# Recurrence with attention: both gates as separate tanh of ScalarE on the weighted sums

## The reference, cut to what matters

```python
def step(h, x_t):                                   # h: [B, 128], 512 steps in order
    combined = concat([h broadcast, enc_hiddens])   # [B, 77, 256]
    score = tanh(combined @ W_att) @ V_att          # [B, 77]
    attn = softmax(score)
    context = attn @ enc_hiddens                    # [B, 128]
    gz, gr, gh = split(concat([x_t, context]) @ Wi + b, 3)
    rz, rr, rh = split(h @ Uh, 3)
    z = sigmoid(gz + rz);  r = sigmoid(gr + rr)
    hh = tanh(gh + r * rh)
    return z * h + (1 - z) * hh
```

## Time and profile before

| | before |
|---|---|
| median of 3 runs | 4724.2 us |
| the profiled execution | 4725.9 us, span of the core 4724.1 us |
| the recurrence in it | from about 324 us to about 2353 us |
| TensorE busy | 4135.0 us, 88% |
| VectorE busy | 2861.7 us, 61% |
| ScalarE busy | 2329.2 us, 49% |
| GpSimd busy | 913.8 us, 19% |

### The profile page before, as it was taken

The page is one execution under the profiler, slowest core; times in us unless marked ns, Lnnn a source line. Parts: engine busy times, 40 slices in busy tenths (PEclk is TensorE's granted clock), DMA queues, the critical chain, the costliest instruction groups (busy, mean ns, idle before and its releaser), DMA issues. The chain is left out here.

```text
span 4724.1 us, 82263 instructions
## 1 busy us (share of the span) xinstructions
PE 4135.0 (88%) x25322; PEld 2378.3 (50%) x25322; DVE 2861.7 (61%) x13564; ACT 2329.2 (49%) x6588; POOL 913.8 (19%) x4350
## 2 busy tenths in 40 slices
PE   6789999999999999999898999678888888888788
PEld 2247777777777777777732334222333323333223
DVE  4546666666666666666654444546666667666323
ACT  3335655555565556565533334224555544455433
POOL 0123333333333333333231000200011000000002
PEclk8889999999999999999999999768888888888889
DMA  0000000000000000000001000011112111211000
GB/s 9 24 7 2 2 2 2 2 2 2 2 2 2 2 2 2 2 2 2 20 16 46 0 1 1 29 59 43 53 46 64 54 60 52 64 45 44 14 17 5
DMA packets 48983, 94.51 MB, mean 20 GB/s; under 512 B 11440, under 2 KB 31936, under 8 KB 48288
## 3 DMA queue, kind: packets, MB, share of 16 engines
q1 hardware_dynamic: 48544, 89.24, 5.9%
HBM read 72.89 MB, written 15.39 MB: 19 GB/s over the span
## 5 line engine op out<-in xcount | busy, mean ns | idle before, releaser
L761 PE MATMUL ps<-g_h,w_p 128*128 128x128 f32 x4096 | 918.6, 306 | 0.0
L2138 ACT ACTIVATE t_ex<-ps 128x1024 f32<-128x1024 f32 (+1 forms) x480 | 471.9, 1021 | 570.8 <-PE ps L2085 557.1
L761 PEld LDWEIGHTS ps<-g_h,w_p 128*128 128x128 f32 x4096 | 618.0, 191 | 0.0
L757 PE MATMUL ps<-g_h,w_p 128*128 128x77 f32 x2048 | 456.7, 304 | 169.7 <-DVE g_h L829 141.0
L2233 DVE TENSOR_REDUCE t_ncol<-ps 128x1 f32<-128x512 f32 x768 | 486.6, 684 | 152.7 <-PE ps L2058 152.2
L825 DVE SCALAR_TENSOR_TENSOR g_used<-g_encg,g_e 128x77 f32<-128x77 f32 x3072 | 550.8, 230 | 0.0
L795 ACT ACTIVATE g_th<-ps 128x77 f32<-128x77 f32 x1024 | 241.4, 236 | 527.5 <-PE ps L757 527.5
L871 POOL TENSOR_SCALAR g_z<-g_tzr 128x1 f32<-128x1 f32 x1024 | 194.9, 190 | 1414.9 <-ACT g_tzr L804 1414.9
L757 PEld LDWEIGHTS ps<-g_h,w_p 128*128 128x128 f32 x2048 | 305.3, 188 | 305.8 <-DVE g_h L829 298.5
L776 PE MATMUL ps<-g_th,g_vrep 128*128 128x77 f32 x2048 | 456.7, 305 | 0.5 <-ACT g_th L795 0.5
L834 DVE TENSOR_REDUCE g_ntop<-ps 128x1 f32<-128x77 f32 x1024 | 244.6, 239 | 337.1 <-PE ps L776 336.3
(11 more groups left out here) (429 smaller groups left out, 6855.9 us busy)
## 6 DMA issues: line engine op xcount, KB each, us to landing
t_qst<-t_turn_q SPq DMA_DIRECT2D x288, 96.0 KB
t_kst<-t_turn_k SPq DMA_DIRECT2D x144, 96.0 KB
t_turn_q<-t_part SPq DMA_DIRECT2D x24, 384.0 KB, 2.5
t_turn_k<-t_part SPq DMA_DIRECT2D x12, 384.0 KB, 3.3
t_wf<-in_t_wf SPq DMA_DIRECT2D x6, 514.5 KB, 5.5
m_experts<-in_experts SPq DMA_DIRECT2D x1, 3072.0 KB, 13.2
t_wa<-in_t_wa SPq DMA_DIRECT2D x6, 448.0 KB, 3.3
t_wx<-in_t_wx SPq DMA_DIRECT2D x6, 448.0 KB, 4.2
```

The source lines that it names most:

```text
L757: M(att[c], w["att_h"], h[t % 2][:, c:c + 1].broadcast_to([P, S]), start=False, stop=True, skip_group_check=True).then_inc(*st.sem("att", c))
L761: return M(G[c][:, g], weights, h[t % 2][:, c:c + 1].broadcast_to([P, P]), start=False, stop=last, skip_group_check=True)
L2138: A(ex[0:kw, slot[pf, c, l, n]], ps[0:kw, at:at + 2], ACT.Exp, scale=SCALE).then_inc(*st.sem(f"{pf}e{n}", c))
```

## The change

In the loop VectorE no longer forms `zr`. ScalarE copies the two gates' parts from PSUM, halved, into the tile `zr` right behind each exp. After the sums it computes each gate by a tanh of its own, with the reciprocal as scale and the halved part as bias, straight from `mac`: first r, then z. For the halves to agree, `encg` of the two gates is scaled by 0.5 before the loop. GpSimd's factors wait for the tanh of z, the candidate for that of r. The order of the lanes in every queue is as before.

```diff
-                        V.tensor_copy(encg[:, g, c], ps[:, 4 * c + 1, 0:S]).then_inc(*pre.sem(f"c{g}_s", c))
+                        V.tensor_scalar(encg[:, g, c], ps[:, 4 * c + 1, 0:S], 0.5 if g < 2 else 1.0, None, ALU.mult)\
+                            .then_inc(*pre.sem(f"c{g}_s", c))
@@ exp(c, t), behind the ACTIVATE of the exp
+                    act.wait_ge(*st.at("gates", c, t))
+                    A(zr[:, c], G[c][:, 0:2, 0], ACT.Copy, scale=0.5).then_inc(*st.sem("gs", c))
@@ candidate(c, t)
-                    act.wait_ge(*st.at("zr", c, t))
-                    A(tzr[:, c], zr[:, c], ACT.Tanh, scale=0.5).then_inc(*st.sem("tzr", c))
+                    act.wait_ge(*st.at("gs", c, t))
+                    act.wait_ge(*st.at("sinv", c, t))
+                    act.wait_ge(*st.at("r", c, t))
+                    A(tzr[:, c, 1:2], mac[:, c, 1:2], ACT.Tanh, bias=zr[:, c, 1:2], scale=sinv[:, c:c + 1]).then_inc(*st.sem("tr", c))
+                    act.wait_ge(*st.at("z", c, t))
+                    A(tzr[:, c, 0:1], mac[:, c, 0:1], ACT.Tanh, bias=zr[:, c, 0:1], scale=sinv[:, c:c + 1]).then_inc(*st.sem("tz", c))
                     act.wait_ge(*st.at("in", c, t))
-                    act.wait_ge(*st.at("tzr", c, t))
+                    act.wait_ge(*st.at("tr", c, t))
                     A(hh[:, c:c + 1], G[c][:, 2, 1:2], ACT.Tanh, bias=hin[:, c:c + 1], scale=tzr[:, c, 1:2])\
                         .then_inc(*st.sem("cand", c))
@@ mix(c, t)
-                    dve.wait_ge(*st.at("gates", c, t))
-                    dve.wait_ge(*st.at("z", c, t))
-                    fma("zr", c, zr[:, c], mac[:, c, 0:2], sinv[:, c:c + 1], G[c][:, 0:2, 0])
+                    dve.wait_ge(*st.at("gs", c, t))
                     dve.wait_ge(*st.at("hm", c, t))
                     fma("in", c, hin[:, c:c + 1], mac[:, c, 2:3], sinv[:, c:c + 1], G[c][:, 2, 0:1])
@@ factors(c, t)
-                    pool.wait_ge(*st.at("tzr", c, t))
+                    pool.wait_ge(*st.at("tz", c, t))
```

More of the change, by code:

```diff
@@ L741, in gru_stage @@
         G = [ps[:, 3 * c + 2, 0:3 * P].rearrange("p (g n) -> p g n", n=P) for c in range(B)]
-        st = Steps(k, "g", 2, pe="att score gates", act="tanh exp tzr cand",
-                   dve="top sinv r z hm zr in h", pool="z1 omz zh saved")
+        st = Steps(k, "g", 2, pe="att score gates", act="tanh exp gs tr tz cand",
+                   dve="top sinv r z hm in h", pool="z1 omz zh saved")
         with nc.Block() as block:
```

## The result

The changed kernel takes 4975.2 us (median of 4 runs, 4969.3 to 4975.4) against 4726.9 us of the kernel before (4 runs, three of them those behind the 4724.2 above); the ratio is 1.0522, 95% interval 1.0504 to 1.0540. Forecast were 4970 us and a range of 4900 to 5085.

A forecast was written before the change was run, and what follows sets the result against it. A chain of latencies, not TensorE, was taken to bound the kernel at 3.94 us per step; afterwards a loop across the lanes at 4.42. (4.42 - 3.94) x 512 = +246, 4724 + 246 = 4970 us, range 4900 to 5085.

The forecast's parts named there:

- Where the bound is now: Recurrence before the change: a chain of latencies through each lane, 3.94 us per time step, bounds it, not TensorE's 3.64.
- slack third loop: ScalarE's queue before the change: one lane's tanh frees the other's gates; two halves of 1.76, 3.52 per step, slack by 0.42.
- A lane's own chain of 3.90: One lane after the change, from attention matmul to its next: 3.90 us against 3.94, alone a gain of 0.04.
- The two tanh: ScalarE's gates: each tanh takes 0.375 us, the second starts 0.275 after the first, the first 0.14 after the attention tanh.
- The last leg: From the end of the gates' tanh through GpSimd's z1 and zh and VectorE's h to the next attention matmul: 0.94 us.
- The new bound: Loop across the lanes through ScalarE's queue after the change: halves of 2.21 us, 4.42 per time step.
- hin near 1208.38, not last: VectorE's input to the candidate: loses 0.13 behind zr, gains waits for hm and the copy, keeps its place, never last.
- TensorE's idle: In the recurrence after the change: TensorE's idle grows to some 0.4 us per lane and step.
- A: Rival: quick small tanh on ScalarE, each lane's own chain binds, loop 3.80 below 3.94, time 4652 us; 5%.
- C: Rival: ScalarE's Copy needs another table, two loads of 1.283 us per lane and step add 2600 us; 1%.
- D: Case: each met wait ahead of the tanh of r costs 0.05; half 2.31, +350, 5074 us; part of the forecast's case.
- B: Rival: TensorE's granted clock falls to 1.2 GHz through idle gaps, 7.28 per step, 6434 us or anything between; 4%.

The follow-up runs named there:

- the last run above: Version against the kernel before: weighted sums take the gate's part as scalar from PSUM, one tanh for both gates, no zr, no copy; 4706.3 us, ratio 0.9943.
- a half of 2.99: Changed kernel with each lane's gates and candidate ahead of the other lane's attention tanh in ScalarE's queue; 5769.4 us, ratio 1.2197.
- the two doses between the gates: Changed kernel with an extra unused tanh between the tanh of r and of z: operands from tiles 5378.2 us, constants 5121.9 us.
- the remedies: Changed kernel with the tanh of z first, 4892.1 us; also z's sum first, 4889.3; also a shortened GpSimd part, 4890.5.

## Why the prediction was right, by its own steps

The number is 0.1% off, and not because errors cancelled: the terms held one by one.

- *Where the bound is now* held: a chain of latencies, and with it the slack third loop. That the loop is there in the kernel before, and how slack, was shown by the extra tanh in that kernel: 2 x 2.029 = 4.06 per step with 0.28 added to each half, so 3.50 without it, where the prediction has 3.52. A lane's own chain of 3.90 cannot be read in the changed kernel, since the queue hides it; if a sum that has been read needs 0.10 to ScalarE, as in the last run above, and not 0.03, it is about 3.97, still far below 4.43.
- *The copy costs 0*: shown alone, 0.9998. It takes 0.16 and not 0.2.
- *The two tanh*: 377 and 375 ns where 0.375 was taken, 0.28 apart (0.275), 0.13 behind the attention tanh (0.14). The nearest row, hh at 351, would have been the lesser choice; 204 plus twice 90 was near. The prediction's estimates from the Trainium skill's figures ("ScalarE: Activation LUTs", "What ACT_TABLE_LOAD costs") are 373 and 280, and the trace agrees with both. For hh, which has the same two operands but its input in PSUM, the same figures give 373 as well, and the traces have 351 before and 336 after.
- *The last leg* of 0.94 is 0.94 (1208.04 to 1208.98): 0.08 to z1 in place of 0.10, and 0.29 twice and 0.28 for the rest.
- *The new bound*: half 2.21 forecast; 2.21 in the timeline, 2.216 in the mean with the few longer halves. 2 x 2.21 against 3.94 is +246; the span grew by 249.
- *hin near 1208.38, not last*: it starts 0.73 after the reciprocal (1207.36 against 1206.63), where 0.71 was its place. It waits 0.12 behind the read of hm's accumulator. No effect.
- *TensorE's idle*: 0.40 per lane and step, as said.

Of the rivals, A (quick small tanh) is refuted by 377 ns. C (table loads) did not happen: the loop has its one load of before. D (waits cost) is refuted by the 0.13 behind the tanh with three waits ahead. B happened in the changed kernel only in traces: two falls of some 7 us, which cost about 2 us together, and 1.00 elsewhere in the loop. But the runs showed it close by: 0.09 more in each half brought the clock to 0.90 on average, 0.28 more to 0.70 to 0.79, and at a half of 2.99 it is 0.50 throughout. The prediction's ground against B, that gaps of 0.3 were harmless before, says nothing of gaps of 0.4, so that the clock held was not foreseen from rows, and there is luck in it. Its price for B was too high: it doubled 1.82 to 3.64 per lane, and at the lower level TensorE's work for one lane took 2.66. The range's upper part (halves of 2.3 and more) was priced at full clock and would have been too low there: at a half of 2.305 the range's sum gives +92 over this result, and 147 was measured. The Trainium skill ("TensorE: Matmul & The Clock Gate", "A second HAM failure mode: psum-queue depth-cycling"), which the prediction weighed, describes this back and forth; the traces of the two doses between the gates show it, and this trace only in its two short falls.

The misses lie in the expectations for the remedies. They followed the chain that was last and put the candidate 0.28 behind the tanh of r, the distance between instructions that do not read each other. But it reads the result of that tanh, and so waits for its whole length and 0.09 more (0.46).

## What to carry to other kernels

In a loop of several independent chains on in-order queues, look for a second kind of cycle beside each chain's own: what one chain's instruction waits behind in a shared queue, followed until it comes back. An instruction that becomes ready earlier gains nothing if it stands in the queue behind one of another chain that is later, and whatever is lengthened behind that point counts once per chain. When one instruction is split into two in a row, name the reader of each result; one of the readers is always second. A reader starts behind the whole length of what it reads, on the same engine too; only an instruction that does not read the one before it starts at the shorter distance.

## What the runs showed of the hardware that was not expected

- A weighted sum on VectorE whose scalar operand is a column in PSUM and which adds where the other multiplied takes 294 ns in place of 230, and the distance to the next grows from 0.16 to 0.22. The two were not tried apart.
- A GpSimd tensor_scalar on one column takes 0.34 us with both scalars from a tile, 0.19 with constants.
- From the end of hh on ScalarE to h on VectorE it is 0.15 us (1207.05 to 1207.20), from the exp's accumulator read to the reciprocal 0.04 (1207.63 to 1207.67 in the kernel before). Why the two differ was not tried.
- A tanh with scale and bias from tiles takes 375 to 377 ns with its input in SBUF, and hh, of the same form with its input in PSUM, 336 in the changed kernel.
- The granted clock switched between its two levels within a steady loop, in turns of some 7 to 30 us. At full clock TensorE was without work for 0.5 and 0.7 us per half there (2.31 and 2.49 less its 1.82). In the changed kernel, with 0.40 in each 2.21, it fell twice in 2270 us, for some 7 us, each time behind one of eight waits of 0.65 or more.
- At the lower level TensorE's work for one lane takes 2.66 us, against 1.82 at full clock: not twice as much.
